# A gated cross-attention and mixture-of-experts block on one core: v of six groups of heads projected ahead by block products and kept in DRAM, scores two heads ahead

## The reference, cut to what matters

```python
B, LQ, LK, D, H, DH = (8, 128, 128, 512, 32, 128)      # 8 x 128 = 1024 tokens
x  = rmsnorm(layernorm(hidden)) * ln_weight
h_q = x @ w_q.T;  h_k = ctx @ w_k.T;  h_v = ctx @ w_v.T   # [1024, 512] @ [512, 32*128] each
score = softmax(where(mask, h_q h_k^T + position_bias[h], -inf))   # per batch and head
attn  = score @ h_v
x1 = x0 + tanh(g) * (layernorm(x0) + attn @ w_out.T)
x2 = x1 + tanh(g2) * (routed experts, two of 16, + shared expert)(layernorm(x1))
```

## Time and profile before

| what | value |
|---|---|
| time, median of 3 runs | 987.17 us (986.87 to 989.12) |
| profiled execution: time, and its span | 987.9 us, 986.2 us |
| TensorE busy | 957.9 us, 97% |
| VectorE, ScalarE, GpSimd busy | 622.7, 402.8, 256.3 us |
| DMA | 160.20 MB, mean 162 GB/s |
| k and q steps | from 8.6 to 323.3 us |
| heads and their filling | from 323.3 to about 808 us |

### The profile page before, as it was taken

One profiled execution on the slowest core, in us unless ns is written; L12 is line 12 of the kernel. 1 busy time (PEld: TensorE's weight loads), 2 busy tenths in 40 slices (PEclk: granted clock), 3 DMA queues, 4 the chain that ended last, 5 costly groups with the idle time before them and its releaser, 6 DMA issues.

```text
span 986.2 us, 13781 instructions
## 1 busy us (share of the span) xinstructions
PE 957.9 (97%) x4915; PEld 798.6 (81%) x4915; DVE 622.7 (63%) x996; ACT 402.8 (41%) x1006; POOL 256.3 (26%) x242
## 2 busy tenths in 40 slices
PE   6999999999999999999999999999999999999994
PEld 5888888888888888888888888888888877777772
DVE  6877669667655357666755667556675597843321
ACT  5336554333332355353452534525345244324442
POOL 1353334343432112110111101101011002053364
PEclk9999999999999999999999999999999999999997
DMA  6645454666665334132331323313233239565589
GB/s 250 222 175 203 170 201 154 224 227 224 210 219 181 142 134 165 60 134 88 134 118 62 134 89 134 119 61 134 89 134 121 100 136 362 184 228 176 172 188 240
DMA packets 68627, 160.20 MB, mean 162 GB/s; under 512 B 7728, under 2 KB 28464, under 8 KB 66384
## 3 DMA queue, kind: packets, MB, share of 16 engines
q1 hardware_dynamic: 61008, 143.99, 40.9%
q0 software_dynamic: 4784, 12.58, 5.5%
q10 hardware_dynamic: 2768, 2.75, 0.8%
HBM read 104.97 MB, written 54.33 MB: 162 GB/s over the span
## 4 chain that ended last, share of the span: by engine, by line
PE 71%; DVE 5%; DMA 2%; ACT 2%; issue 1%; POOL 1%; SPq 0%; DVEq 0%; ACTq 0%
PE ps_job L673 11%; PE ps_job L675 11%; PE ps_job L674 11%; PE ps_score L810 6%; PE ps_attn L838 5%; PE ps_attn L1068 5%; PE ps_turn L824 3%; PE ps_job L1077 2%; PE ps_attn L715 1%; PE ps_attn L716 1%; PE ps_attn L717 1%; DMA y_slots<-y_out 1%; PE ps_turn L1052 1%; PE ps_score L715 1%; DMA w_raw<-wa_dram 1%
## 5 line engine op out<-in xcount | busy, mean ns | idle before, releaser
L597 POOL TENSOR_TENSOR score_bias<-mask_bias,pos_bias 128x1024 f32<-128x1024 f32 x32 | 76.8, 2399 | 394.5 <-DVE probs L1537 378.4
L1123 ACT ACTIVATE probs<-probs,neg_max 128x128 f32<-128x128 f32 x256 | 99.4, 392 | 71.4 <-DVE neg_max L1540 71.4
L673 PE MATMUL ps_job<-wv_hi,ctx_lo 128*128 128x512 f32 x256 | 101.1, 395 | 0.0
L675 PE MATMUL ps_job<-wv_hi,ctx_hi 128*128 128x512 f32 x256 | 99.8, 390 | 0.0
L674 PE MATMUL ps_job<-wv_lo,ctx_hi 128*128 128x512 f32 x256 | 99.7, 389 | 0.0
L1537 DVE TENSOR_TENSOR probs<-ps_score,score_bias 128x512 f32<-128x512 f32 x64 | 43.9, 685 | 74.8 <-PE ps_score L810 70.6
L1113 ACT ACTIVATE pT<-ps_turn 128x512 f32<-128x512 f32 x64 | 35.1, 596 | 118.3 <-PE ps_turn L824 118.3
L1113 ACT ACTIVATE v_s<-ps_job 128x512 f32<-128x512 f32 x64 | 38.2, 597 | 88.1 <-PE ps_job L675 88.1
L1563 DVE TENSOR_TENSOR acc<-ps_job,acc 128x512 f32<-128x512 f32 x56 | 38.6, 690 | 55.0 <-PE ps_job L675 54.2
L577 POOL TENSOR_TENSOR w_sum<-w_raw 128x256 f32<-128x256 f32 x30 | 24.0, 800 | 180.9 <-PE ps_score L717 69.1
L1068 PE MATMUL ps_attn<-ew_s,xbT 128*128 x248 | 62.3, 380 | 0.9 <-ACT xbT L1113 0.9
(11 more groups left out here) (406 smaller groups left out, 2328.9 us busy)
## 6 DMA issues: line engine op xcount, KB each, us to landing
kq<-st SPq DMA_DIRECT2D x32, 1024.0 KB, 4.2
kq_s<-kq SPq DMA_DIRECT2D x64, 512.0 KB, 4.5
w_raw<-wa_dram SPq DMA_DIRECT2D x31, 512.0 KB, 5.8
y_slots<-ones SPq DMA_DIRECT2D x32, 256.0 KB, 4.9
wv_raw<-wv_dram SPq DMA_DIRECT2D x8, 1024.0 KB, 5.0
ew_s<-ew_dram SPq DMA_DIRECT2D x4, 2048.0 KB, 14.2
y_slots<-y_out SPq DMA_DIRECT2D x31, 256.0 KB, 2.8
wo_raw<-wo_dram SPq DMA_DIRECT2D x7, 1024.0 KB, 4.7
```

Source lines behind the costliest of these rows:

```text
L597: nc.gpsimd.tensor_tensor(score_bias[:], mask_bias[:], pos_bias[:, i % 2].unsqueeze(1).broadcast_to([P, B, P]), ALU.add).then_inc(bias_rea ...
L673: nc.tensor.matmul(psum, l_lo, r_hi, start=(k == 0), stop=False)
L675: last = nc.tensor.matmul(psum, l_hi, r_hi, start=False, stop=(closed and k == n - 1))
L1123: last = nc.scalar.activation(probs[:, half, b], probs[:, half, b], ACT.Exp, bias=neg_max[:, half, b:b + 1], accum_out=row_sum[:, half, b: ...
```

## The change

- v of groups 0 to 5 is projected right after q, as three pairs of groups. A pair has 4 steps (`v_step(u, n)`), each for two token tiles and 1024 output columns, by seven products of 6 matmuls (`project_v_seven`); here the tokens are the stationary operand. The weights of a pair come in by `load_wv` (2 MB), their sums are made by VectorE for pair 0 (`sum_wv_first`) and by GpSimd for pairs 1 and 2 (`sum_wv`, four operations of 1024 columns), the high parts by ScalarE (`high_wv`), the low parts by VectorE in place of the raw ones (`low_wv`). The result is stored into the DRAM tensor `v_all` (`store_v`), and each group's v is loaded before it is needed (`load_v`, 2 MB, two buffers).
- v of groups 6 and 7 stays plain: 16 tiles, 5 before the first head (`AHEAD`), 11 beside the heads of group 0 (`FILL`). They go through a tile of two slots (`v_out`) to `v_all` as well (`keep_v`, 256 KB each).
- Each head is followed by two tiles of the output projection of the group before, instead of four in half of the heads.
- `score(i + 2)` stands where `score(i + 1)` stood; `probs`, `neg_max` and `row_sum` have two buffers. Weights of the output projection have two buffers and are split in the second head of a group.
- The residual adds come after head 31's `take_attn_lo`; x is loaded again earlier.

```diff
+KQ = H
+PAIRS = NG // 2 - 1
+STEPS = KQ + BH * PAIRS
+ORDER = (A11, S2, S1, S3, A12, S4, A22)
+AHEAD = range(5)
+FILL = (range(5, 8), range(8, 11), range(11, 14), range(14, 16))
...
+            def load_v(g):
+                if g < 2 * PAIRS:
+                    for n in range(BH - 2, BH):
+                        s = v_step(g // 2, n)
+                        sp.wait_ge(kq_stored[s % 2], stores(s))
+                else:
+                    for n in range(2):
+                        sp.wait_ge(v_kept[n], 16 * B)
+                if g:
+                    sp.wait_ge(v_in, 16 * g)
+                sp.dma_start(v_s[g % 2][:], v_all[g].rearrange("t p k -> p t k")).then_inc(v_in, 16)
+            def keep_v(m):
+                sp.wait_ge(v_sbuf, m + 1)
+                sp.dma_start(v_all[2 * PAIRS + m // B, m % B], v_out[:, m % 2]).then_inc(v_kept[m % 2], 16)
...
+            for s in range(KQ):
...
                 store_kq(s)
+                if s == KQ - 2:
+                    sp.wait_ge(a_psum, prod(s, 7))
+                    load_wv(0)
...
+            for u in range(PAIRS):
+                for n in range(BH):
+                    if n == 0 and u + 1 < PAIRS:
+                        sp.wait_ge(a_psum, prod(v_step(u, 0) - 1, 7))
+                        sp.wait_ge(wv_split, 7 * (u + 1))
+                        load_wv(u + 1)
...
+                    store_v(u, n)
             sp.wait_ge(a_psum, prod(STEPS - 1, 7))
-            sp.dma_start(wv1_raw[:], wv[1]).then_inc(wv_in, 16)
+            load_v(0)
+            sp.wait_ge(wv_last_split, 1)
+            load_wv_last(1)
+            load_wo(0)
             for i in range(H):
                 g, j = divmod(i, G)
                 if i + 2 < H:
...
+                if i == 1:
+                    load_v(1)
+                if i < G:
+                    for m in (AHEAD, FILL[0], FILL[1], FILL[2])[i]:
+                        keep_v(m)
+                if i == G:
+                    for m in FILL[3]:
+                        keep_v(m)
+                if j == 0 and g:
+                    if g + 1 < NG:
+                        sp.wait_ge(attn_psum, 2 * i)
+                        load_v(g + 1)
+                    if g == 1:
+                        sp.wait_ge(v_psum, 2 * B)
+                    else:
+                        sp.wait_ge(o_psum, B * (g - 1))
+                    load_wo(g)
...
+            def sum_wv(u):
+                raw, n = v_raw[u % 2], 4 * u
+                pool.wait_ge(wv_in, 64 * (u + 1))
+                nc.gpsimd.tensor_tensor(raw[S1][:], raw[S3][:], raw[A22][:], ALU.add).then_inc(wv_summed, 1)
...
...
+            def project_v_seven(u, n):
...
+                def one(psum, place, block, left, fresh):
+                    if n == 0:
+                        pe.wait_ge(wv_split, 7 * u + place + 1)
...
+                pe.wait_ge(a_act, act_took(s - 2, 2))
+                one(first, 0, A11, tokens(0, 0), True)
...
+                pe.wait_ge(a_dve, dve_took(s, 2))
+                one(third, 5, S4, tokens(1, 1), False)
...
             score(0)
-            for t in range(B):
-                project_v(0, t)
+            for m in AHEAD[:-2]:
+                project_v(m)
+            score(1)
+            for m in AHEAD[-2:]:
+                project_v(m)
             for i in range(H - 2):
                 g, j = divmod(i, G)
                 turn_probs(i)
-                score(i + 1)
+                score(i + 2)
                 attend(i)
...
+            def take_v(m):
+                act.wait_ge(v_psum, m + 1)
+                if m >= 2:
+                    act.wait_ge(v_kept[m % 2], 16 * (m // 2))
+                copy(v_out[:, m % 2], ps_job[m % 2][:]).then_inc(v_sbuf, 1)
...
+            act.wait_ge(kq_stored[(STEPS - 1) % 2], stores(STEPS - 1))
+            for m in AHEAD:
+                take_v(m)
+                if m in (1, 3):
+                    exps(0, m // 2)
+            exps(1, 0)
+            for i in range(H):
+                g = i // G
+                if i == 0:
+                    exps(1, 1)
                 take_pT(i)
...
+            def low_wv(u, k):
+                block = ORDER[k]
+                dve.wait_ge(wv_summed, 4 * (u + 1))
+                dve.wait_ge(wv_hi_done, 7 * u + k + 1)
+                V.tensor_tensor(v_lo[u % 2][block][:], v_raw[u % 2][block][:], hi_of(u, k)[:], ALU.subtract)\
+                 .then_inc(wv_split, 1)
...
+                if s == KQ - 1:
+                    sum_wv_first()
+                    low_wv(0, 0)
+                if s == KQ:
+                    low_wv(0, 5)
+                    low_wv(0, 6)
+                if s >= KQ:
+                    u, n = divmod(s - KQ, BH)
+                    if u and n == 0:
+                        low_wv(u, 6)
+                    if u + 1 < PAIRS:
+                        for k in ((), (0,), (1,), (3,))[n]:
+                            low_wv(u + 1, k)
...
+                if s == KQ - 1:
+                    low_wv(0, 1)
+                    low_wv(0, 2)
```

More of the change, by code:

```diff
@@ L113, in build @@
         ctx_lo = place("ctx_lo", [P, C, T], F32R, at_ctx_lo)
[L114 to L119, removed]
+        at_ct = room(2 * C * T * 4)
         at_xT = room(2 * C * T * 4)
@@ L449, in store_kq, with store_v, load_wv, load_wv_last @@
                     sp.wait_ge(a_dve, dve_took(s, 5))
+            def store_kq(s):
+                which, pair = divmod(s, KQ // 2)
+                stepped(s)
                 sp.dma_start(kq[which, 2 * pair:2 * pair + 2].rearrange("h p t -> p h t"), st[:, s % 2])\
                   .then_inc(kq_stored[s % 2], 16)
+            def store_v(u, n):
+                s = v_step(u, n)
+                stepped(s)
+                for r in range(2):
+                    sp.dma_start(v_all[2 * u + r].rearrange("(c n) p k -> n p c k", c=2)[n],
+                                 st[:, s % 2, r].rearrange("p (c k) -> p c k", c=2)).then_inc(kq_stored[s % 2], 16)
+            def load_wv(u):
+                for r in range(2):
+                    for d in range(2):
+                        block = ((A11, A12), (S3, A22))[r][d]
+                        sp.dma_start(v_raw[u % 2][block][:], wv[2 * u + r][:, HALF_C * d:HALF_C * (d + 1)])\
+                          .then_inc(wv_in, 16)
+            def load_wv_last(n):
+                sp.dma_start(wv_last_raw[n][:], wv[2 * PAIRS + n]).then_inc(wv_last_in, 16)
             def load_kq(i):
-                s = STEPS // 2 + i // 2
-                sp.wait_ge(kq_stored[s % 2], 16 * (s // 2 + 1))
+                s = KQ // 2 + i // 2
+                sp.wait_ge(kq_stored[s % 2], stores(s))
                 for which in range(2):
@@ L590, in _ @@
                     to_minus_half(rms[:], rms[:], 2)
+            for u in range(1, PAIRS):
+                sum_wv(u)
             pool.wait_ge(mask_done, 1)
@@ L823, in turn_probs @@
                     for b in range(BH):
-                        last = nc.tensor.transpose(ps_turn[half][:, cols(b)], probs[:, half, b], ident[:])
+                        last = nc.tensor.transpose(ps_turn[half][:, cols(b)], probs[i % 2][:, half, b], ident[:])
                     last.then_inc(pT_psum, 1)
@@ L1108, in _ @@
         def _(act):
-            for n, k in enumerate((A11, 3)):
-                act.dma_start(w_raw[:, 0, k], wa[0, :, k]).then_inc(first_w_in[n], 16)
+            for k in (A11, 3):
+                act.dma_start(w_raw[0][:, k], wa[0, :, k]).then_inc(first_w_in, 16)
             def copy(dst, src):
@@ L1528, in _ @@
                     V.tensor_tensor(c21, fourth[:], su[:, p], ALU.add).then_inc(a_dve, 1)
+                if s == KQ - 1:
+                    low_wv(0, 1)
+                    low_wv(0, 2)
+                if s >= KQ:
+                    u, n = divmod(s - KQ, BH)
+                    if u + 1 < PAIRS:
+                        for k in ((), (), (2,), (4, 5))[n]:
+                            low_wv(u + 1, k)
             def bias_and_max(i):
                 if i == 0:
-                    dve.wait_ge(kq_stored[1], 16 * (STEPS // 2))
+                    dve.wait_ge(kq_stored[STEPS % 2], stores(STEPS - 2))
                 dve.wait_ge(bias_ready, i + 1)
```

457 lines of the change are left out of this document (260 added, 197 removed).

## The result

The changed kernel takes 1023.0 us (median of 4 runs, 1020.6 to 1025.4), the kernel before 987.0 (4 runs, 986.6 to 989.1): ratio 1.036, 95% interval 1.0331 to 1.0389. It is slower, as forecast, but by 36 us where the forecast was 15, and above the range of 988 to 1011. The profiled execution took 1023.7 us for a span of 1021.9.

A forecast was written before the change was run, and what follows sets the result against it. The prediction took TensorE, busy 99.8 to 100% in the touched stages, as the bound. Waits of 33.3 us (A to E) against a gain of 18.1 made +15.2, so 1002 us, with 988 to 1011 for 8 in 10.

The forecast's parts named there:

- gain: TensorE work saved: 72 fewer matmuls for v, 16.3 us, and scores two heads ahead, 1.8 us; 18.1 us together.
- A: Entry into v: TensorE waits for the first pair's load, sums and low parts, plus some half clock; 11.0 us.
- B: Third steps of pairs 0 and 1: evictions wait behind the next pair's load and GpSimd's sums; 6.1 us.
- C: Entry into the attention: fifth v tile waits for a store behind 6.3 MB, exps and slow matmuls follow; 9.9 us.
- D: Remaining heads: lateness after the wo split, 1.4 us, and head 7's late keys, 3.3 us; 4.7 us.
- E: Tail: residual adds now come after the last `take_attn_lo`, delaying the first final add; net 1.6 us.
- the 1.4 us behind the wo split: Heads after the wo split: VectorE is 3.5 us late and `take_pT` waits behind an exp; 1.4 us in all.
- the clock: TensorE runs at half clock after idling: 2.4 us extra, booked as 1.0 at v's entry and 2.0 at the attention's.
- B's transfer: Weight load of the second pair of v, 2.1 MB, was to land 7.3 us after its issue.
- (2): Stores of v don't wait behind loads: 991, chance 0.09; with B at its lower end 987, another 0.09.
- (3): Transfers land side by side, so waits are 11.8 us and the kernel gets faster: 981; chance 0.09.
- (4): GpSimd at 3.0 us a sum and VectorE past 9.9 us per head, both late: 1018; chance 0.11.

The follow-up runs named there:

- x_warm: Changed kernel with idle 512-column matmuls put in front of its six long TensorE waits: 1011.3 us, 1.0262 of the kernel before.
- x_kq_first: Changed kernel with 2 MB of v, output weight, residual and last two v-tile stores issued behind the next head's keys: 1010.3 us, 1.0236 of the kernel before.
- x_keep_act: Changed kernel with group 0's v tiles stored from ScalarE's own DMA queue instead of SyncE's: 1010.4 us, 1.0239 of the kernel before.
- x_all: Changed kernel with four edits: v stores by ScalarE, low parts one step later, keys first, first pair's load ahead of the store: 990.8 us, 1.0017.
- x_order: x_all with keys of heads 2 and 3 issued ahead of the last value weight, wo and the second v: 990.9 us, 1.0015 of the kernel before.
- x_all_warm: x_all with 17 idle matmuls in front of step 32's first product: 989.9 us, 1.0007 of the kernel before.
- x_best: x_order with 17 idle matmuls at step 32's first product and 8 in the tail's wait: 989.8 us, 0.9998 of the kernel before.
- x_ahead_plain: x_order with seven v tiles ahead of head 0 instead of five: 994.9 us, 1.0046 of the kernel before.

## Why the prediction was wrong

Each term: forecast, then idle time plus half clock in the changed kernel's trace.

| term | forecast | measured |
|---|---|---|
| gain | 18.1 | heads at 9.91 as forecast; the rest not measured alone |
| A, first pair | 11.0 | 9.0 + 3.2 = 12.2 |
| B, later pairs | 6.1 | 10.3 + 3.8 = 14.1 (by its cure 15.6) |
| C, entry to the attention | 9.9 | 10.1 + 1.8 = 11.9 (cure 12.6: with head 7, less the two waits that came up) |
| D, other heads | 4.7 | 9.1 + 3.4 = 12.5 (by its cure 12.7) |
| E, tail | 1.6 | 2.0 - 1.4 + 1.7 = 2.3 |
| half clock at 896 us, cause open | none | 1.7 |
| net | +15.2 | +36.6 by these, +36 by the runs |

The mechanisms were mostly right: every wait that was named is in the trace at its place, with the releaser that was named, but for the 1.4 us behind the wo split; head 31's wait was not named. Sizes were wrong, by 21 us in all: 12.5 are half clock and the rest waits, above all B and D.

- **The step that failed most is the clock.** The prediction says "After an idle stretch TensorE is slow", has the price from the start of the kernel (2.4 us), and then books it in A ("Here half of it hides behind VectorE: 1.0") and in C (2.0) only. B, head 7 and the tail carry none. Measured are 15.5 us (1.7 of them the open stretch at 896 us), 12.5 more than booked, and `x_warm` took 11.7 of them away with nothing but idle matmuls. A price that in this execution follows each of the seven new waits was charged to two. It is no constant: behind A's wait of 8.4 us it was 3.1 us in the changed kernel and 1.9 in `x_kq_first` (from 326 to 338 us, 7.20 x 0.43 and 6.64 x 0.28), and the changed kernel's own four executions have mean clocks from 0.972 to 0.979.
- **B's transfer**: "It lands 7.3 us later (2.1 MB)" took bytes over 400 GB/s. It landed after 10.4, with four issues of 0.46 us each and 1 MB of stores beside it. VectorE's wait of 12.1 us passed most of the 3.1 on to TensorE (5.8 where 3.3 was forecast), and the second pair likewise (4.5 for 2.8).
- **D**: head 7 had the right cause, SP's wait for `keep_v(15)` (`x_keep_act`: 0.6 us without it), but was sized at 3.3 and measured 6.3; head 31, whose keys took 11.97 us and cost 2.7 of wait and 1.4 of half clock, wasn't looked for at all. "The other moved loads (kq, pos, wo, x_res) lie under TensorE's heads at a DMA share of 0.31 and cost nothing" is the sentence that is wrong: x_res and wo, 3 MB, stand ahead of the keys in one ring, and a low mean share doesn't help what is queued behind them. The 1.4 us for the wo split did not appear.
- **A and C** were sound: the 11.0 and 9.9 stand beside 12.2 and 11.9. C's cause (the store of a v tile behind 6.3 MB in SP's ring) is shown by `x_keep_act`. That the two stand close is in part luck: A's idle time was forecast 1 us too long and its half clock 2.2 too short.
- **Rivals**: (2) and (3) are out by the landings, 15.1 us for 256 KB. (4), GpSimd and VectorE too slow, would have given 1018, nearer to the result, but by luck: the sums took 2.40 and heads 9.91.

Left open: why the granted clock falls at one place some 54 us behind the tail's wait in five of the changed versions (896 us in the changed kernel, 881 in `x_kq_first`, 862 in `x_all` and `x_order`, 860 in `x_all_warm`), and not before or in the others. In four of these five the tail's own wait has no half clock behind it. In the same stretch, with the same short waits of 0.6 and 0.3 us, the windows are, before and then in `x_order`:

```profile
855.00:865.00 10.00, 9.16 (x49) 7.42 (x50) 6.41 (x10) 4.80 (x11) 2.31 (x2) 1.00 0.92 321
```

```profile
855.00:865.00 10.00, 9.11 (x40) 7.26 (x40) 6.84 (x11) 4.23 (x9) 2.04 (x2) 0.84 0.88 299
```

It costs 9.11 x 0.16 = 1.5 us. With 8 idle matmuls in the tail's wait (`x_best`) it is not there, but it is not there in `x_ahead_plain` either, which has none; no run tells its cause apart.

## What to carry to other kernels

Charge a new wait of TensorE twice: once for its length and once for the half clock behind it, 1.4 to 3.2 us each in the changed kernel. Behind the new waits of 3.1 us and more it came in every trace here, behind those of about 2 us only in some. Where a wait can't be removed, idle matmuls in it win the second part back. In a ring that serves several consumers, list for each transfer the megabytes ahead of it at its own deadline, stores and residuals included; a mean DMA share of 0.31 says nothing about that. And don't put a wait for a slow helper (here VectorE's for GpSimd's sums) in front of evictions that release TensorE: one step later was worth 15.6 us at no cost.

## What the runs showed that I had not expected

- A wait of 2.0 us at the tail can have half clock behind it (0.57 in 842 to 846 us), but had it in only five of the ten traces with that wait.
- A store of 256 KB takes 15.1 us in SP's ring, 7.1 in ScalarE's own beside the same load, so a second queue is worth 8 us there, but not the whole; and 5.5 us of other waits came up at the entry once the old one was gone.
- At the entry to the attention the wait moved, over five versions, from the keys to the probabilities, to head 0's attend, and to a bank of the v tiles, within 1% of the same time, with the DMA engines full at about 400 GB/s for 25 us. Five orders of the work did not beat it; whether fewer bytes there would, no run shows.
